# One-core quaternion attention in a six-stage transformer kernel: row statistics of the side jobs handed out one tile a turn

## The reference

```python
x = x + _L1_attn_ref(_layernorm(x, axis=-1), ...)      # 4 batches of 1024 tokens, 16 heads of 16
#   q, k = quat_norm(quat_linear(x, ...)); v = quat_linear(x, ...)
#   scores = einsum('bthd,bshd->bhts', q, k) * 0.25 + const
#   out = quat_linear(einsum('bhts,bshd->bthd', softmax(scores), v), oW, ob)
x = x + 0.5 * _L1_ffn_ref(_layernorm(x, axis=-1), ...)
#   affinity = sinkhorn(x @ gate_query.T / temp, 6 rounds); then top-k tokens of each expert
```

## Time and profile before

| | us |
|---|---|
| median of 3 runs | 2972.54 |
| lowest and highest | 2971.9 and 2976.63 |
| the profiled execution, its own time | 2977.58 |
| its span in the trace | 2975.8 |
| first exponential of the loop's turn 0 | 2092.11 |
| last exponential of turn 255, start | 2693.7 |

### The profile page before, as it was taken

The page is one execution under the profiler, slowest core; times in us unless marked ns, Lnnn a source line. Parts: engine busy times, 40 slices in busy tenths (PEclk is TensorE's granted clock), DMA queues, the critical chain, the costliest instruction groups (busy, mean ns, idle before and its releaser), DMA issues.

```text
span 2975.8 us, 55341 instructions
## 1 busy us (share of the span) xinstructions
PE 2806.7 (94%) x22765; PEld 2198.6 (74%) x22765; DVE 1855.6 (62%) x3753; ACT 1633.4 (55%) x2460; POOL 539.4 (18%) x478
## 2 busy tenths in 40 slices
PE   8999999997999999999999977998899999998998
PEld 7788999996767768889999955996333434333898
DVE  7675555547877676755555477876534464436776
ACT  4334455543543444345555433775688878892676
POOL 0001132312000000011423144553000000001343
PEclk9999999998999999999999989999999999998999
DMA  4223343323000012122433244774442252523675
GB/s 145 68 64 95 93 99 77 87 75 92 3 3 23 3 61 75 64 89 85 103 85 89 75 146 126 199 199 110 106 128 51 52 126 58 123 42 115 181 202 143
DMA packets 237852, 279.70 MB, mean 94 GB/s; under 512 B 23811, under 2 KB 219040, under 8 KB 237600
## 3 DMA queue, kind: packets, MB, share of 16 engines
q1 hardware_dynamic: 205296, 228.75, 26.5%
q0 software_dynamic: 30720, 45.85, 8.0%
q10 hardware_dynamic: 1584, 1.57, 0.2%
HBM read 204.58 MB, written 72.88 MB: 93 GB/s over the span
## 4 chain that ended last, share of the span: by engine, by line
PE 69%; DVE 18%; ACT 5%; issue 4%; DMA 2%; POOL 1%; DVEq 0%; POOLq 0%; ACTq 0%
PE PS L162 16%; PE PS L163 15%; PE PS L164 15%; PE PS L2914 12%; PE PS L1003 6%; PE PS L170 2%; DVE SM L194 1%; DVE FW L612 1%; DVE PROD L604 1%; ACT FW L540 1%; DVE FHH L607 1%; ACT FHH L534 1%; ACT Z L573 1%; DVE SM L1378 1%; PE PS L496 1%
## 5 line engine op out<-in xcount | busy, mean ns | idle before, releaser
L3064 ACT ACTIVATE P<-PS 128x1024 f32<-128x1024 f32 x512 | 484.8, 1047 | 99.7 <-PE PS L2914 98.0
L162 PE MATMUL PS<-FH,FW 128*128 128x366 f32 (+1 forms) x1408 | 509.6, 362 | 12.3 <-ACT SIL L530 6.0
L163 PE MATMUL PS<-FH,FW 128*128 128x366 f32 (+1 forms) x1408 | 501.7, 356 | 0.0
L164 PE MATMUL PS<-FH,FW 128*128 128x366 f32 (+1 forms) x1408 | 499.4, 355 | 0.0
L534 ACT ACTIVATE FHH<-PROD 128x366 fp32r<-128x366 f32 (+1 forms) x352 | 195.4, 555 | 531.1 <-DVE PROD L604 531.1
L607 DVE TENSOR_TENSOR FHH<-PROD,FHH 128x366 fp32r<-128x366 f32 (+1 forms) x352 | 209.9, 596 | 218.7 <-ACT FHH L534 218.7
L162 PE MATMUL PS<-FW,FHH 128*122 128x256 f32 (+1 forms) x1184 | 341.2, 288 | 1.5 <-DVE FHH L607 1.5
L163 PE MATMUL PS<-FW,FHH 128*122 128x256 f32 (+1 forms) x1184 | 335.5, 283 | 0.0
L164 PE MATMUL PS<-FW,FHH 128*122 128x256 f32 (+1 forms) x1184 | 335.3, 283 | 0.0
L604 DVE TENSOR_TENSOR PROD<-SIL,PS 128x366 f32<-128x366 f32 (+1 forms) x352 | 206.8, 587 | 153.4 <-PE PS L164 151.9
L162 PEld LDWEIGHTS PS<-FH,FW 128*128 128x128 f32 x1408 | 267.0, 190 | 36.6 <-ACT SIL L530 10.6
(11 more groups left out here) (458 smaller groups left out, 5589.5 us busy)
## 6 DMA issues: line engine op xcount, KB each, us to landing
WS<-L_ffn_w_dram SPq DMA_DIRECT2D x256, 256.0 KB, 3.8
WST<-L_ffn_W_dram SPq DMA_DIRECT2D x168, 256.0 KB, 3.5
S<-parts_scratch SPq DMA_DIRECT2D x60, 384.0 KB, 8.1
parts_scratch<-PT SPq DMA_DIRECT2D x28, 512.0 KB, 4.0
WST<-L_ffn_W1s_dram SPq DMA_DIRECT2D x40, 256.0 KB, 3.0
WST<-L_ffn_W3s_dram SPq DMA_DIRECT2D x40, 256.0 KB, 3.5
WST<-L_ffn_W2s_dram SPq DMA_DIRECT2D x40, 256.0 KB, 4.0
xa_scratch<-X SPq DMA_DIRECT2D x17, 512.0 KB, 5.2
```

The lines of the kernel that those rows point to most:

```text
L162: e.matmul(o, lh, rh, start=start, stop=False, skip_group_check=True)
L163: e.matmul(o, ll, rh, start=False, stop=False, skip_group_check=True)
L164: return e.matmul(o, lh, rl, start=False, stop=stop, skip_group_check=True)
L3064: e.activation(self.PR[K % 3][:, 2 * jj:2 * jj + 2, :].rearrange("p a b -> p (a b)"), c.pair(2 * ((2 * K + jj) % 3)), ACT.Exp, scale=0.25) ...
```

## The change

It has three edits. In prep the statistics of a batch are handed out one tile a turn for eight turns instead of two tiles a turn for four, the root follows in the ninth turn, and the first `zz` one turn behind the root instead of five (the same turn as before). In sink_stats the batches 0 and 1 get one tile a turn, batch 2 stays at two. In order() a turn may begin one job at most whose first item is a `root` or a `zz`. No instruction is added or removed.

```diff
     def prep(self, b):
         n, q = self.call, Jobs()
-        for i in range(0, 8, 2):
-            q.add(1, ("stats", n, "p", b, i), ("stats", n, "p", b, i + 1))
+        for i in range(8):
+            q.add(1, ("stats", n, "p", b, i))
         q.add(1, ("root", n, "p", b))
-        q.add(5, ("zz", n, b, 0))
+        q.add(1, ("zz", n, b, 0))
         q.add(1, ("zz", n, b, 1), ("xb", n, b))
...
     def sink_stats(self, q, b, turn, h):
-        for i in range(4 * h, 4 * h + 4, 2):
-            q.add(1, *[("stats", self.call, b, b, i + x) for x in range(2)])
+        each = 2 if b == 2 else 1
+        for i in range(4 * h, 4 * h + 4, each):
+            q.add(1, *[("stats", self.call, b, b, i + x) for x in range(each)])
...
     def order(self):
-            used = False
+            used = rows = False
             for q in (rest, fin, *turns):
                 while q.open(K):
                     items = q.jobs[0][1]
+                    if items[0][0] in ("root", "zz"):
+                        if rows:
+                            break
+                        rows = True
```

## The result

The changed kernel takes 2976.88 us (median of 22 runs) against 2971.86 for the kernel before (22 runs beside them): ratio 1.0015, interval 1.0008 to 1.0022, so 4.5 us slower (2.4 to 6.5). That is under the 0.2% (5.9 us) taken beforehand as the line of what can be told from no change, but the interval lies clear of zero: with 22 runs of each a small slowdown can be told, and 0.2% was too coarse a line. The forecast was 2.9 us slower.

A forecast was written before the change was run, and what follows sets the result against it. TensorE, or in turns without a side job ScalarE, sets the pace; VectorE has idle time. Terms +0.5 + 2.7 + 1.9 - 2.8 - 1.6 = +0.7, plus stretches 1.45 and 0.7, give +2.9: 2975.4 us, range 2967.5 to 2979.8.

The forecast's parts named there:

- the stretches counted at A and C: New half-clock stretches of TensorE behind new waits: one in turns 1 to 14, 1.45 us; half in turns 129 to 141, 0.7.
- more than 1 us outside the loop: Sign that the prediction is wrong: a difference of over 1 us outside the fifth layer's loop.
- Site A: Turns 1 to 14, batch 1: smaller waits and a half-clock stretch gone, against a later root's new waits; net +0.5 us.
- Site B: Turns 64 to 80, batches 0 and 2: waits of 0.95 and 3.7 in place of 1.66; net +2.7 us.
- 2 x 2.4: Two roots at 2.4 us each in VectorE's 10.2 us queue from 2272.95 to the first `ht` eviction.
- Site C: Turns 129 to 141, batch 3: gain 0.6, loss 2.5 from the root ahead of `sk`'s reciprocal; net +1.9 us.
- Site D: Turns 142 to 146, batch 1's statistics: wait of 1.69 shrinks to 0.55, half-clock stretch goes; -2.8 us.
- Site E: Turns 88 and 160: `pj` with `sq` no longer delays the copy of bank 6 by 0.8; both go, -1.6 us.
- The limit: One `root` or `zz` job a turn changes nothing, cost 0; a misread order would mean 1.8 us at most.
- Only the gains are real: Rival: VectorE finds room for the roots in the loop, so -7.5 us, 2965.0; chance 0.12.
- Nothing moves: Rival: work changes places in VectorE's queue, but waits come from stores or ScalarE; time stays 2972.5; chance 0.13.
- The new waits drag the clock down: Rival: two half-clock stretches at each of turns 12 to 14, 76 to 79, 137 to 141; +7.9, 2980.4; chance 0.13.

The follow-up runs named there:

- after: First profile of the changed kernel, all three edits on the kernel before; 2976.88 us, ratio 1.0015.
- after_again: Second profile of the unaltered changed kernel; loop 602.4 us.
- no_limit: The changed kernel without its third edit, the limit of one root or zz job a turn; 2977.35 us, ratio 1.0019.
- before: First profile of the kernel before, without any of the edits; median 2971.86 us, loop 601.6.
- sink_only: Only the edit in sink_stats (batches 0 and 1 one tile a turn) on the kernel before; 2974.32 us, ratio 1.0013.
- sink_again: The edit in sink_stats alone on the kernel before, run a second time; 2977.23 us, ratio 1.0008.
- prep_only: Only the edit in prep (statistics one tile a turn, root in the ninth turn) on the kernel before; 2978.85 us, ratio 1.0022.
- xb_end: The changed kernel with GpSimd's additions moved to the end of prep's queue in program order; they ran when they always did; 2980.61 us, ratio 1.0020.
- xb_wait: The changed kernel with GpSimd's additions at the end of prep's queue and made to wait for their batch's last p3; 2973.89 us, ratio 1.0002.
- before_again: Second profile of the unaltered kernel before; loop 600.2 us.
- root_only: The kernel before with only prep's root moved to the ninth turn, statistics still two tiles a turn; 2982.85 us, ratio 1.0042.
- best: The kernel before with regrouped prep tiles, earlier zz of batches 2 and 3, and only batch 1's sink_stats one tile a turn; 2969.01 us, ratio 0.9990.

## Why the prediction was right, point by point

- **The whole.** Forecast +2.9 us and no change that can be told; measured +4.5 (2.4 to 6.5), under the line of 5.9 but clear of zero. By the profiles of the same order (after, after_again, no_limit) the loop is 603.5 on average against 600.9, +2.6. That the sum came so near is partly luck: the stretches counted at A and C, 2.15 us, cost nothing in most executions (1.4 in after), the loss at B was 2.4 us larger than forecast, and the two nearly cancel. The mechanism of losses and gains held; sizes did not all hold. The sign "more than 1 us outside the loop" can't be read: outside the loop single executions of one order differ by up to 7 us.
- **Site A**, forecast +0.5, with a stretch +1.95. Four profiles have the order of before in these turns (43.1, 43.0, 42.4 and 42.6, with sink_only and sink_again) and six the changed one (44.7, 42.5, 42.9, 42.8, 43.8 and 42.9, with prep_only, xb_end and xb_wait): +0.5 on average, in a scatter of 2 us. The waits of 0.84 and 2.05 came as forecast (0.9 and 1.9). The second transpose waits at most 2.05, not 2.4: 2131.35 + 2.4 is 2133.75, not the 2134.0 that I had worked with. The wait of turn 14, 0.37 to 1.56 behind an eviction that in before_again waits for a store, is gone, a gain that I had not counted. The gain of 1.45 for the stretch behind `sta` is in good part chance: only one of the four profiles has it. Its size was right there (1.46), but a stretch costs less where VectorE, not TensorE, is the late one, because it fills the wait. 0.6 of the 44.7 is a turn 1 at half clock, the end of the stretch with which every version enters the loop.
- **Site B**, with the first half of E: forecast +2.7 - 0.8 = +1.9, measured +4.3 over the turns 64 to 128. The step that failed is the size of one term, "2 x 2.4" for the two roots: one of them takes 4.86 beside GpSimd. Without that (xb_wait) the same turns are 159.3, +1.5, and the waits are 0.93 and 3.51 where I had 0.95 and 3.7.
- **Site C**, forecast +1.9 and half a stretch: measured +1.9 (30.9 to 32.8) with full clock in all profiles of the changed order; prep_only has a half-clock stretch there and takes 32.8 all the same. The waits were 1.65, 0.21, 0.75 and 1.26 for the 1.7, 1.05 and 1.3 I had worked out.
- **Site D**, forecast -2.8: measured -2.9 against the first profile before and -1.8 against the second, which had no stretch there. The wait is 0.34 where 0.55 was expected.
- **Site E**, -0.8 for each half: the waits for the copy in turns 90 and 162 are gone. Turns 147 to 185 are 1.1 shorter; the root of turn 150 costs nothing that shows.
- **The limit** costs and gives nothing, as argued from the table of turns (no_limit).
- **The rivals.** "Only the gains are real" falls with prep_only and root_only. "Nothing moves" falls. "The new waits drag the clock down" came true in part: a half-clock stretch of 6.8 us lies at B in every profile with the changed order and GpSimd's additions beside the root, and at A in one (after), never at C. It did not bring its price: at B TensorE was busy for 3.87 of the 6.80 us, at A for 5.97, and there the stretch cost 1.4.

```profile
2124.70:2131.50 6.80, 5.97 (x28) 1.84 (x28) 4.86 (x9) 3.22 (x4) 5.28 (x6) 0.50 0.62 248
2281.80:2288.60 6.80, 3.87 (x16) 1.41 (x16) 4.38 (x8) 1.94 (x2) 2.71 (x4) 0.50 0.06 19
```

- **Half-clock stretches.** Against the forecast they did not hang on the length of a wait alone: C's 1.65 left the clock at 1.00 in the changed kernel, and so did both waits of 2.05 in after_again. The window after A's waits and a window of C in the changed kernel:

```profile
2128.40:2131.80 3.40, 3.40 (x16) 1.35 (x16) 1.38 (x2) 1.58 (x2) 3.09 (x5) 0.53 0.24 95
...
2434.00:2437.40 3.40, 3.19 (x31) 1.10 (x32) 3.16 (x11) 2.51 (x3) 0.00 (x0) 1.00 0.00 0
```

The page "TensorE: Matmul & The Clock Gate" of the Trainium skill (section "HAM oscillation — how this bites in real kernels") would have had no stretch behind waits as short as these; the runs have them in some executions and not in others of the same order, so neither its rule nor mine settles it. The sum without the stretches at A and C, which the prediction put near +0.4, is +0.7 by its own terms.

## What to carry to other kernels

Handing out side work evenly is good only as long as the last piece, on which others wait, does not move with it: here eight tiles in eight turns put a chain of 12 dependent instructions, 2.4 us, right in front of its readers, and a chain twice as long where GpSimd was at work. Place the end of such a chain first, in a stretch where its engine idles (the timeline shows it as the idle time before the next wait), and spread only what lies before it. An instruction moved in the program's order stays where it was if its engine has nothing else queued; to move it in time it needs a wait.

## What the runs showed of the hardware

- VectorE instructions on 128x8 elements took 0.17 us alone and, every second one, 0.57 to 0.60 beside GpSimd's additions of 128x256; a root took 4.86 to 4.87 in six profiles with the additions beside it from its start, 4.08 in best, where they ended midway, and 2.39 in xb_wait, where they were moved away. The additions of batch 2 took 0.73 us each with the root beside them (after) and without (before, xb_wait). The Trainium skill's "GPSIMD Engine Reference", section "1. Specifications", says that GpSimd's SBUF interfaces are shared with VectorE, with contention for VectorE instructions in a 2-port performance mode or with two SBUF inputs; that section gives no price. The trace agrees that the two get in each other's way, and here the price was a factor of 2 on a chain. L208 waited too, with one tensor as its input; whether it ran in such a mode no run here shows. Evictions of 128x512 from PSUM beside the additions kept their 0.69.
- The same order of instructions gives the same waits within 0.02 us where no store is waited for, while a wait behind a store moved from 0.37 to 1.56 between two executions and a half-clock stretch changed the waits beside it (2.05, 0.82 and 0.50 in turn 13).
